# Two transformer layers on one core: heads weighed by key tiles, second projections and the third FFN layer at other places

## The reference, cut

```python
x = L0_attn_x                                   # (8, 512, 128) float32
xn = _layernorm(x)
x = x + L0_attn(xn) + L0_ffn(xn)
xn = _layernorm(x)
x = x + L1_attn(xn) + L1_ffn(xn)

# L0_attn, 16 heads of 8, h = rmsnorm(x, norm_w); q, k, v = h @ Wq, h @ Wk, h @ Wv
# linear: scores of Taylor features of q @ Wqf, k @ Wkf, causal, divided by their row sums + eps
# sliding window: scores = q.k / sqrt(8), allowed t-64..t, softmax, times v
out = concatenate([lin, win]) @ Wout
# L0_ffn, widths 128 -> 512 -> 512 -> 512 -> 128
h = silu(x @ w1.T * w1_s) * (x @ w2.T * w2_s)
h = gelu(h @ h1.T * h1_s)
h = gelu(h @ h2.T * h2_s)
return h @ w3.T * w3_s
# L1_attn: layernorm, q, k, v with biases, causal softmax(q.k / sqrt(8)) v, 16 heads, @ Wo + bo
# L1_ffn: 8 experts, each token's best two, gelu between, weighed by a softmax over the two
```

## Time and profile before

| | us |
|---|---|
| median of 3 runs (1579.31 to 1579.46) | 1579.32 |
| the profiled execution | 1584.48 |
| its span | 1582.7 |
| TensorE busy | 1363.4 |
| VectorE busy | 823.8 |
| ScalarE busy | 708.2 |
| GpSimd busy | 601.5 |

### The profile page before, as it was taken

How to read it: one execution, slowest core, us unless ns; L and a number is a source line. 1 busy time by engine, 2 the same in 40 slices (tenths; PEclk the granted TensorE clock), 3 DMA queues, 4 the chain that set the end, 5 groups by cost and what they waited for, 6 DMA issues and landing times.

```text
span 1582.7 us, 28933 instructions
## 1 busy us (share of the span) xinstructions
PE 1363.4 (86%) x9122; PEld 933.8 (59%) x9122; DVE 823.8 (52%) x3372; ACT 708.2 (45%) x1503; POOL 601.5 (38%) x791
## 2 busy tenths in 40 slices
PE   5979878998899789988998899988997885679997
PEld 2555546655565556555656465556555664449997
DVE  3063375436653566347634764366536644826653
ACT  2345236523662356235643364236623640237765
POOL 6123233323341433233413342223414342618787
PEclk9989999997999899989998899979999995679999
DMA  9204400332022302240034004310233004204443
GB/s 264 60 2 113 108 16 7 96 86 62 7 75 65 104 9 68 54 119 10 30 93 114 14 4 120 84 40 7 75 87 82 7 8 149 85 18 62 62 63 48
DMA packets 82248, 102.09 MB, mean 65 GB/s; under 512 B 12473, under 2 KB 43105, under 8 KB 82017
## 3 DMA queue, kind: packets, MB, share of 16 engines
q1 hardware_dynamic: 63616, 86.53, 19.8%
q0 software_dynamic: 14304, 10.61, 4.3%
q10 hardware_dynamic: 4176, 3.01, 0.7%
HBM read 55.44 MB, written 46.37 MB: 64 GB/s over the span
## 4 chain that ended last, share of the span: by engine, by line
PE 62%; DVE 14%; issue 12%; ACT 5%; DMA 3%; POOL 2%; SPq 2%; DVEq 0%; POOLq 0%; ACTq 0%
PE bank L543 14%; PE bank L549 14%; PE heads L606 13%; PE bank L532 6%; PE bank L528 3%; PE bank L853 3%; PE bank L861 3%; DVE xnT_s L1279 2%; ACT probs L920 2%; DVE hrow L1279 2%; PE bank L647 2%; DVE hT_s L1279 2%; DVE mx_c L1279 1%; PE bank L537 1%; SPq L427 1%
## 5 line engine op out<-in xcount | busy, mean ns | idle before, releaser
L920 ACT ACTIVATE probs<-bank 128x512 f32<-128x512 f32 (+2 forms) x896 | 444.6, 578 | 489.4 <-PE bank L549 487.4
L549 PE MATMUL bank<-K,Q 128*128 128x192 f32 (+4 forms) x1024 | 243.9, 335 | 48.0 <-DVE attn L1320 13.7
L1079 POOL TENSOR_SCALAR_AFFINE_SELECT probs<-probs 128x384 f32<-128x384 f32 x256 | 127.7, 521 | 390.3 <-ACT probs L920 356.2
L606 PE MATMUL heads<-probs,V 128*9 128x192 f32 (+4 forms) x3072 | 225.4, 441 | 19.9 <-issue 14.3
L549 PE MATMUL bank<-Q,K 128*128 128x192 f32 (+4 forms) x1024 | 220.4, 329 | 25.3 <-DMA Q<-mrow_s 11.2
L549 PEld LDWEIGHTS bank<-K,Q 128*128 128x128 f32 x1024 | 181.5, 209 | 93.9 <-issue 30.6
L549 PEld LDWEIGHTS bank<-Q,K 128*128 128x128 f32 x1024 | 156.2, 201 | 59.0 <-issue 25.1
L549 PE MATMUL bank<-QM,K 128*128 128x512 f32 (+3 forms) x512 | 145.0, 379 | 44.7 <-DVE gatesT_s L1257 14.2
L606 PEld LDWEIGHTS heads<-probs,V 128*9 128x9 f32 x3072 | 81.0, 97 | 152.9 <-issue 120.0
L1141 POOL DMA_INDIRECT out<-h1T_s x78 | 124.0, 1589 | 54.0 <-ACT h1T_s L1033 27.6
L910 ACT ACTIVATE probs<-bank,sh_s 128x512 f32<-128x512 f32 x64 | 44.0, 687 | 207.9 <-PE bank L543 207.9
(11 more groups left out here) (186 smaller groups left out, 2091.6 us busy)
## 6 DMA issues: line engine op xcount, KB each, us to landing
Q<-slots_of_q SPq DMA_DIRECT2D x16, 1024.0 KB, 10.6
K<-slots_of_k SPq DMA_DIRECT2D x64, 192.0 KB
QM<-slots_of_qm SPq DMA_DIRECT2D x8, 1024.0 KB, 8.7
slots_of_q<-Q SPq DMA_DIRECT2D x24, 256.0 KB, 3.0
slots_of_k<-QM SPq DMA_DIRECT2D x24, 256.0 KB, 4.0
slots_of_qm<-Q SPq DMA_DIRECT2D x24, 256.0 KB, 4.1
slots_of_q<-probs SPq DMA_DIRECT2D x24, 256.0 KB, 3.0
slots_of_k<-probs SPq DMA_DIRECT2D x24, 256.0 KB, 3.7
```

The costliest lines, as they stand in the source:

```text
L549: mm = pe.matmul(to[:, at:at + right.shape[1]], left, right, start=True, stop=True, skip_group_check=True)
L606: mm = pe.matmul(heads[ROWS * i:ROWS * i + D + 1, P * j:P * j + widths[j]], V[:, j, HG * g + i, :], slot_of(kind, 2 * g + i // 2)[:, at:at ...
L920: return act.activation(to, bank, func, scale=scale, bias=bias).then_inc(taken_sem(run, unit), 1)
L1079: pool.affine_select(out=three, in_=three, compare_op=ALU.is_ge, fill=0.0, base=0, pattern=[[0, 3], [1, P]], channel_multiplier=-1)
```

## The change

- `weigh` takes a list of key tiles, and the waits stand at tile 0 only. Triangle groups 0 to 2 are weighed one key tile behind each of four successive score units (16 to 19, 26 to 29, 36 to 39); LIN group 3 behind causal units 7 to 10; CAUSAL group 3 behind window units 6 to 9; SLIDE groups 0 to 2 in two halves. SLIDE group 3, and the tail's last group, stay whole.
- Copies, turns and divides behind them move back by one to three units. In slide_stage PE turns causal group 3 after unit 12 (10 before) and `attn` after 15 (13 before, now behind the eight `gate`/`up` products); DVE copies causal group 3 at n = 10, behind `split_lo` of q1 and k1 (8 before, ahead of them).
- In dense_stage `hT2`, `xnT2`, `q2`, `k2` come right behind `h2_1`; then `logits`, `v2`, `h2_2`. `h2_3` goes behind linear unit 5, `third_layer` behind linear unit 9 (with its addition on DVE ahead of the maxima), `prefix` from linear unit 5 to 3.
- The halves of q2 and k2 lie in Q1 in place of `probs`; SP fetches q1 only when q2 has landed, and ACT no longer waits for the sending.

The core of the diff; the lists of units at the top change in step, and the tail is called with the new tables.

```diff
-LIN_WEIGH, LIN_TURN = {16: 0, 26: 1, 36: 2}, {23: 0, 33: 1}
-CAUSAL_WEIGH, CAUSAL_TURN = {16: 0, 26: 1, 36: 2}, {23: 0, 33: 1}
-SLIDE_WEIGH, SLIDE_TURN = {12: 0, 20: 1, 28: 2}, {17: 0, 25: 1}
+
+TRI_WEIGH = {16 + 10 * g + n: (g, tiles) for g in range(G - 1) for n, tiles in enumerate(((0,), (1,), (2,), (3,)))}
+LIN_TURN = {23: 0, 33: 1}
+CAUSAL_TURN = {24: 0, 34: 1}
+SLIDE_WEIGH = {12 + 8 * g + n: (g, tiles) for g in range(G - 1) for n, tiles in enumerate(((0, 1), (2, 3)))}
+SLIDE_TURN = {18: 0, 26: 1}
+LAST_LIN = {7 + n: (n,) for n in range(NT)}
+LAST_CAUSAL = {6 + n: (n,) for n in range(NT)}
+LAST_SLIDE = (0, 1, 2, 3)
...
-        units += linear(m) + (["prefix"] if m == 5 and before else [])
+        units += linear(m) + (["prefix"] if m == 3 and before else []) + (["h2_3"] if m == 5 else []) + (["third_layer"] if m == 9 else [])
...
-    units += ["h2_1", "h2_2"] if after else []
-    units += ["hT2", "xnT2", "q2", "k2"] if this else []
-    units += ["h2_3"] if after else []
-    units += ["v2", "logits"] if this else []
-    units += ["third_layer"] if after else []
+    units += ["h2_1"] if after else []
+    units += ["hT2", "xnT2", "q2", "k2", "logits", "v2"] if this else []
+    units += ["h2_2"] if after else []
...
-                    "q2": halves2[0], "k2": halves2[1]}
+                    "q2": (Q1[:, 0, :], Q1[:, 1, :]), "k2": (Q1[:, 2, :], Q1[:, 3, :])}
...
+                    if this:
+                        sp.wait_ge(S["slots_q2"], due("slots_q2", (b, 0), 16))
+                        sp.sem_inc(S["unread"], 1)
                     fetch_sent((b, 1), "q1")
...
-            def weigh(sequence, kind, g, other=None):
+            def weigh(sequence, kind, g, tiles, other=None):
 
                 V = V2 if kind == CAUSAL else V1
-                if kind == SLIDE:
-                    pe.wait_ge(S["slide_middle"], due("slide_middle", sequence, 2 * g + 2))
-                    pe.wait_ge(S["slide_edge"], due("slide_edge", sequence, 2 * g + 2))
-                else:
-                    pe.wait_ge(S[f"masked{kind}"], due(f"masked{kind}", sequence, 2 * g + 2))
-                if g:
-                    pe.wait_ge(S[f"heads_copied{kind}"], due(f"heads_copied{kind}", sequence, g))
-                elif other:
-                    pe.wait_ge(S[f"heads_copied{other[0]}"], due(f"heads_copied{other[0]}", other[1], G))
+                if tiles[0] == 0:
+                    if kind == SLIDE:
+                        pe.wait_ge(S["slide_middle"], due("slide_middle", sequence, 2 * g + 2))
+                        pe.wait_ge(S["slide_edge"], due("slide_edge", sequence, 2 * g + 2))
+                    else:
+                        pe.wait_ge(S[f"masked{kind}"], due(f"masked{kind}", sequence, 2 * g + 2))
+                    if g:
+                        pe.wait_ge(S[f"heads_copied{kind}"], due(f"heads_copied{kind}", sequence, g))
+                    elif other:
+                        pe.wait_ge(S[f"heads_copied{other[0]}"], due(f"heads_copied{other[0]}", other[1], G))
                 starts, widths, head = (SLIDE_AT, SLIDE_N, NT * WQ) if kind == SLIDE else (TRI_AT, TRI_N, PROBS)
-                for j in range(NT):
+                for j in tiles:
                     for i in range(HG):
                         at = head * (i % 2) + starts[j]
                         mm = pe.matmul(heads[ROWS * i:ROWS * i + D + 1, P * j:P * j + widths[j]],
                                        V[:, j, HG * g + i, :], slot_of(kind, 2 * g + i // 2)[:, at:at + widths[j]],
                                        start=(j == 0), stop=(j == NT - 1), skip_group_check=True)
-                mm.then_inc(S[f"heads_out{kind}"], 1)
+                if tiles[-1] == NT - 1:
+                    mm.then_inc(S[f"heads_out{kind}"], 1)
...
-                    if m in LIN_WEIGH:
-                        weigh(now, LIN, LIN_WEIGH[m], (SLIDE, previous) if before else None)
+                    if m in TRI_WEIGH:
+                        weigh(now, LIN, *TRI_WEIGH[m], (SLIDE, previous) if before else None)
...
-                    if m == 5 and before:
+                    if m == 3 and before:
                         prefix(run, previous)
+                    if m == 5:
+                        dense(run, "h2_3", h2T, hidden_b, 3)
+                    if m == 9:
+                        if not before:
+                            pe.wait_ge(S["w3_scaled"], 1)
+                        third_layer(run)
...
-                    if n == 7:
-                        weigh(now, LIN, 3)
+                    if n in LAST_LIN:
+                        weigh(now, LIN, 3, LAST_LIN[n])
...
-                    if before and n in CAUSAL_WEIGH:
-                        weigh(previous, CAUSAL, CAUSAL_WEIGH[n], (LIN, now))
+                    if before and n in TRI_WEIGH:
+                        weigh(previous, CAUSAL, *TRI_WEIGH[n], (LIN, now))
...
-                    if n == 6 and before:
-                        weigh(previous, CAUSAL, 3)
+                    if n in LAST_CAUSAL and before:
+                        weigh(previous, CAUSAL, 3, LAST_CAUSAL[n])
                     if n == 8 and after:
                         wait_taken(run, "hT1")
                         project(run, "q1", wq[:, :], hT[:, :])
                         project(run, "k1", wk[:, :], hT[:, :])
-                    if n == 10 and before:
-                        turn_heads(run, previous, CAUSAL, 3)
                     if n == 10 and after:
                         project(run, "qm1", wqm[:, :], hT[:, :])
+                    if n == 12 and before:
+                        turn_heads(run, previous, CAUSAL, 3)
                     if n in SLIDE_WEIGH and this:
-                        weigh(now, SLIDE, SLIDE_WEIGH[n], (CAUSAL, previous) if before else (LIN, now))
-                    if n == 13 and before:
-                        turn_attn(run, CAUSAL)
+                        weigh(now, SLIDE, *SLIDE_WEIGH[n], (CAUSAL, previous) if before else (LIN, now))
                     if n == 14 and after:
                         wait_taken(run, "xnT1")
                         for c in range(FC):
                             project(run, f"gate{c}", w1T[:, c * P:(c + 1) * P], xnT[:, :])
                             project(run, f"up{c}", w2T[:, c * P:(c + 1) * P], xnT[:, :])
+                    if n == 15 and before:
+                        turn_attn(run, CAUSAL)
...
-                    dense(run, "h2_2", h2T, hidden_b, 2)
                 if this:
                     pe.wait_ge(S["hrow2"], due("hrow2", now, 1))
                     turn(run, "hT2", lambda t: hrow[:, t, :])
...
                     wait_taken(run, "hT2")
                     project(run, "q2", wq1[:, :], hT[:, :])
                     project(run, "k2", wk1[:, :], hT[:, :])
-                if after:
-                    dense(run, "h2_3", h2T, hidden_b, 3)
-                if this:
-                    project_rows(run, "v2", hT, wv1[:, :])
                     wait_taken(run, "xnT2")
                     project_rows(run, "logits", xnT, wgT[:, :], E)
+                    project_rows(run, "v2", hT, wv1[:, :])
                 if after:
-                    if not this:
-                        pe.wait_ge(S["w3_scaled"], 1)
-                    third_layer(run)
+                    dense(run, "h2_2", h2T, hidden_b, 2)
...
-                    if n in (18, 28):
-                        copy_heads(now, n // 10 - 1)
+                    if n == 5:
+                        gelu(run, "h2_3", hidden_c[3], sh2[:, 3:4])
+                    if n in (20, 30):
+                        copy_heads(now, n // 10 - 2)
...
-                    if n == 9:
+                    if n == 11:
                         copy_heads(now, 3)
...
+                dve.wait_ge(S["xa_ready"], due("xa_ready", now, 1))
+                dve.sem_inc(S["unread"], 1)
+                dve.wait_ge(full_sem(run, "third_layer"), full_at(run, "third_layer"))
+                dve.sem_inc(S["third_added"], 1)
+                dve.tensor_tensor(xs[:, :, :], bank_of(run, "third_layer")[:, :].rearrange("p (t n) -> p t n", n=P), xa[:, :, :], ALU.add)\
+                    .then_inc(taken_sem(run, "third_layer"), 1)
...
-                    if n in (18, 28, 38) and before:
-                        copy_heads(previous, CAUSAL, n // 10 - 1)
+                    if n in (20, 30) and before:
+                        copy_heads(previous, CAUSAL, n // 10 - 2)
...
-                    if n == 36:
+                    if n == 35:
                         negate_max(run, "slide_max", mrow_s)
...
+                if before:
+                    copy_heads(previous, CAUSAL, 2)
...
-                    if n == 8 and before:
-                        copy_heads(previous, CAUSAL, 3)
                     if n == 9 and after:
                         split_lo(run, nxt, "q1")
                         split_lo(run, nxt, "k1")
-                    if n == 12 and before:
```

(19 more changed lines are left out.)

47 lines of the change are left out of this document (21 added, 26 removed).

## The result

The changed kernel takes 1600.24 us (median of 4 runs, 1595.75 to 1607.31) beside 1579.39 before: ratio 1.0126, 95% interval 1.0078 to 1.0174. The sign and the mechanism in the window stage (slide_stage) came out as forecast, and the time lies inside the range; but the loss is 20.9 us where 10.2 were worked out.

What follows compares the result with a forecast made beforehand. TensorE was taken to bound most stages, VectorE the stretch with the maxima. Terms -0.8 - 2.7 + 0.8 + 1.0 + 3.8 gave +2.1 us per steady pass, +10.2 in all: 1589.5 us, 8-in-10 range 1565 to 1604.

Steps and rivals of the forecast that it cites:

- E: Slide_stage: five more trips, a late xn and a stall at causal group 3's turn, +3.8 us a pass, bounds +1.1 and +5.5.
- C: Third group, up to the first causal unit: three more trips between scores and weighing, +0.8 us a pass.
- D: Causal_stage: nine more trips cost +2.5 us, two waits shrink; +1.0 us a pass, bounds 0 and +2.4.
- A: From the mix to the first maximum unit: instructions moved, -0.8 us a pass, bounds -2.4 and +1.1.
- The gap of 2.61 at TensorE's own branch I put at 1.2: Loop's branch: TensorE's wait shrinks to 1.2 us with long h2_2 rows queued behind it, bounds 0.5 and 2.6.
- I keep one: Behind the loop's branch: one stretch at 1.2 GHz stays in each pass.
- Q2 lands earlier: Second queries' transfer, ahead of the first maximum unit: lands sooner, sharing no DMA engines with q1; no time was priced.
- Its 6.6 us: VectorE's late return from its own branch, to be hidden by 7.1 us of TensorE work in h2_3 and third_layer.
- B: The maxima: VectorE starves less behind the first two split weighings, -2.7 us a pass, bounds -2.3 and -4.6.
- rival (1): The clock stays up, so the first two stretches reach their far bounds: -1.4 us a pass, 1568.5 us; chance 0.20.
- Rival (4): Slower still: new stalls in dense_stage and slide_stage bring half clock, 3.4 us a pass more, 1610 us; chance 0.12.
- Rival (2): Trips are free, paid per weighing or hidden in waits: -2.7 us a pass, 1560.7 us; chance 0.12.

Runs made afterwards that it cites:

- x_c3early: Changed kernel with causal group 3's four tiles at window units 4 to 7, ahead of q1 and k1, copy and turns moved along; 0.9988 of the kernel before.
- x_cawhole: Changed kernel with linear group 3 and causal groups 0 to 2 weighed whole again; 0.9940 of the kernel before.
- x_short: x_moved with h2_2 ahead of logits and v2, so short products come last ahead of the loop's branch; 1.0017 of the kernel before.
- x_moved: Changed kernel with all weighings whole at their old places, only the moved work left; 1561.7 us, 0.9884 of the kernel before.
- x_h22: Changed kernel with h2_2 again ahead of the turns of hrow and xn, and h2_3 behind v2; 1.0256 of the kernel before.
- x_pieces: Changed kernel's tiles kept, with h2_2, h2_3, third layer and logits in the old order; 1.0212 of the kernel before.

## Why the prediction was right, and where it was not

**Right: sign, and the reason.** The kernel is slower because tiles among scores cost TensorE more than they save, and most in slide_stage. **E** is +4.1 us for a forecast of +3.8. Idle time in it grew by 2.3 us for a forecast of 2.45: the stall at causal group 3's turn is 1.32 us for 1.35, by the chain that was worked out, and the late `xn` 0.66 on the mean (0.14 to 1.03) for 0.6. x_c3early takes away the first and leaves the second, x_cawhole the other way round. Busy time grew by 1.8 for 1.4. **C** is +0.8 for +0.8; at equal clock it is 0.6 to 0.7 (8.27 to 8.87, 6.65 to 7.35). **D** is +1.1 for +1.0: nine trips of 0.30 us for 0.28, and the three of group 2 at 0.23 each, which were to lie in the wait for the row maxima: that wait is 0.62 us in the pass read closely, for 1.39. Idle time in D fell by 1.9 us in all. So 0.28 for a trip was right.

**A, mis-sized in the direction of a gain: -2.0 for -0.8.** Set side by side, the passes that begin at 498.7 and 508.6 both have one stretch at 1.2 GHz there, as I had it, so that the terms can be read off the idle times: the turns +2.2 (2.74 less the 0.57 that TensorE waited before, ahead of q2, in a row that the earlier trace rows leaves out and that stands below; forecast +3.0), the wait ahead of the first maximum unit -1.7 (forecast -2.2), the gap at the branch -2.5 (forecast -1.4). The step that failed is "The gap of 2.61 at TensorE's own branch I put at 1.2": it is 0.13, and 0.23 on the mean. Its sign was right and its reason too, as x_short shows; that it is worth 4 us a pass once the clock behind it counts (x_short against x_moved), I did not see. On the mean of six passes A's gain is of another make: idle time is only 0.4 us less and busy time 1.6, as 5.3 us less are at 1.2 GHz. The pass that I read had 3.4 us of it in A, the mean 8.1, so "I keep one" undercounted what was there to lose. The step that was missing is the transfer of the second queries: "Q2 lands earlier" was priced at nothing, and it is what ends the stretch, 0.5 to 1.9 us behind TensorE's own work, 1.0 on the mean. So the idle time at the turns was no cost of its own; x_h22 took it away and became slower. "Its 6.6 us", which `h2_3` and `third_layer` were to hide, shrank too, to the 3.03 shown above.

```profile
508.98 1.13 PE L532 MATMUL bank<-hT_s,wq_s 128*128 128x512 f32 x2 [0.57 <-ACT hT_s L910]
```

**B, the term that failed: -2.7, and -0.6 was measured.** The waits themselves were about right (3.3 and 2.3 us for 3.2 and 2.0). But by these forecasts they shrink by 2.35 us, not 2.7, and by the trace by 1.9. Nor do they come through in full: on the mean of six VectorE's idle time in the stretch fell by 1.3 us, and its busy time rose from 27.6 or 28.1 to 28.57 us, 0.7 on the mean, since TensorE gets from the first maximum unit to the gates' turn 0.66 us sooner and VectorE has more of its units still ahead. This 0.66 is part of A's gain. The move has a part in it too: B is 0.6 longer in x_moved than before, and the tiles alone gain 1.9 us there in the old order (x_pieces) and 1.2 beside the moved work. A and B together are -2.6 for a forecast of -3.5. Half clock stayed at the weighings as forecast (8.0 us for 8.4), so rival (1) was near for A and wrong for B.

**The sum.** Six passes give +20.8 us in the profiled runs where 12.6 were forecast, the last pass +3.8 where -0.4 was, and the first and the tail -1.8 where -2 was. Of the last pass's 3.8, some 2.7 are half clock (23.2 us instead of 17.8); why it has more there was not looked into. The profiled run of after lies 7.1 us above its median, that of before 5.2, so that the medians differ by 20.9. Some of the hit is luck: A gained 1.2 us a pass more than forecast and B 2.1 less, which cancel in part, and even so the loss is twice the one forecast. The time lies just under the upper end of the range of 1583 to 1601 that the sum had of its own. Rival (4) foresaw 1610 through half clock behind the new stalls. In dense_stage that came, 3.4 us of it behind the waits at the turns in five of six passes, but the stretches behind the branch went; behind the 1.32 us of slide_stage none follows directly, and over a pass it is 6.8 us less than before. Rival (2), free trips, which term C calls the last rival, is refuted by x_cawhole.

## What to carry to other kernels

An idle engine ahead of a chain that ends last anyway is no cost: before you fill a wait, follow the transfer that the next stage needs, and shorten that first (here a fetch in two halves), then reorder. Split a block of one mode between others only where another engine starves for it; elsewhere each piece pays its trip, and the last piece carries everything that is queued behind it, on every engine. Put the longest instructions, not the shortest, ahead of a loop's branch.

## What the hardware showed that was not expected

The order of three groups of products ahead of the branch moved 22 us (x_moved to x_short). With eight products of 512 columns last, TensorE's gap at the branch is 0.03 to 0.3 us on the mean of six passes; with the third layer's 32 products of 128 columns last it is 1.7 (before), and with eight of 8 and eight of 128 columns last 2.2 (x_short). Behind these gaps, up to the gates' turn, came 8.1 and 6.2 us at a granted clock of 0.5 in the mean pass; with the full queue it was none in after and 0.8 in x_moved, but 4.8 in x_h22, where the wait of 5.1 us for the transfer stands. The waits of 1.4 and 1.3 us ahead of the turns are the same in every kernel that has them, and 0.6 to 2.9 us at 0.5 came behind them.

VectorE's own branch does not cost the same each time. From the branch to its next instruction it was 6.0 to 6.8 us in before, while the DMA engines were busy throughout (share 1.00 from 523.5 to 529.9), 5.4 to 6.0 in x_pieces at a share of 0.7, and 2.8 to 3.3 in after, at a share of about 0.3 (0.27 from 526.6 to 529.4). In x_short both are found: 3.9 to 4.2 us at 0.6 to 0.7 and 7.1 and 8.4 at nearly 1. No run takes the transfers alone away from the branch, so that they are the cause is not shown.

A change between score units and column-tiled weighings costs 0.23 to 0.30 us for the way there and back, once per change, at full clock.
